# Layer 1's products are no longer added in pairs, and the expert work, the scatter's side work and the first steps change their order

## The reference

```python
xn = layernorm(x)
# layer 0: 32 chunks of 16 tokens, one after the other, for 8 x 16 heads
k_h = softmax(k_t @ W_in) * lr ; q_h = softmax(q_t @ W_in)
o_t = q_h @ W_out + (q_h @ k_h.T * mask) @ v_t
W_out, W_in = W_out + k_h.T @ v_t + ..., W_in + ...       # two updates by attention
s = (layernorm(o) * (xn @ Wg)) @ Wo
x = x + s * silu(moe0(xn))                                # top 2 of 8, gated experts
xn = layernorm(x)
# layer 1: state space scan, 256 channels x 16 states n, 8 batch rows of 512 tokens
h = silu(conv4(xn @ W_in)) ; res = silu(xn @ W_res)
dlt, Bm, Cm = split(h @ W_x) ; delta = softplus(dlt @ W_dt + b)
state[n] = exp(delta * A[n]) * state[n] + delta * h * Bm[n]    # along the tokens
y = sum over n of state[n] * Cm[n] + h * D
s = (y * res) @ W_out
x = x + s * silu(moe1(xn))                                # top 2 of 8, relu, capacity 640
```

## Time and profile before

| | |
|---|---|
| median of three runs | 1483.17 us (1479.82 to 1483.81) |
| profiled execution: its time | 1483.56 us |
| its span, first to last instruction | 1481.8 us |
| instructions | 15782 |
| layer 0, attention steps | from 169.60 us to about 800 us |
| layer 1, row 0 to row 7 | from about 879 us to 1451.83 us |

### The profile page before, as it was taken

How to read it: one execution, slowest core, us unless ns; L and a number is a source line. 1 busy time by engine, 2 the same in 40 slices (tenths; PEclk the granted TensorE clock), 3 DMA queues, 4 the chain that set the end, 5 groups by cost and what they waited for, 6 DMA issues and landing times. The chain is left out here.

```text
span 1481.8 us, 15782 instructions
## 1 busy us (share of the span) xinstructions
PE 982.6 (66%) x3548; PEld 573.3 (39%) x3549; DVE 1267.5 (86%) x2435; ACT 706.7 (48%) x1337; POOL 692.2 (47%) x630
## 2 busy tenths in 40 slices
PE   3670125877878787777534675379888898987531
PEld 1140123555555555555324521134434444443200
DVE  5768986999999999999998888399989898899944
ACT  2542212555555455555322263068678576784305
POOL 5003772222222222222110037639888898888770
PEclk9875556889898889988757588579999999999955
DMA  9993111000000000000522133145454453544741
GB/s 369 220 185 54 36 47 25 21 20 21 21 21 18 20 20 20 19 18 11 144 85 57 29 121 124 57 144 163 155 185 167 153 188 125 187 139 151 162 51 57
DMA packets 94436, 141.23 MB, mean 95 GB/s; under 512 B 22068, under 2 KB 66881, under 8 KB 89905
## 3 DMA queue, kind: packets, MB, share of 16 engines
q1 hardware_dynamic: 83696, 118.01, 26.8%
q0 software_dynamic: 10688, 22.67, 5.7%
HBM read 108.02 MB, written 34.74 MB: 96 GB/s over the span
## 5 line engine op out<-in xcount | busy, mean ns | idle before, releaser
L1919 DVE TENSOR_TENSOR ps<-ps,cv 128x512 f32<-128x512 f32 x256 | 162.9, 682 | 27.3 <-ACT ps L1451 27.3
L1034 PE MATMUL ps<-Q,ident 128*128 128x512 f32 x256 | 143.7, 654 | 49.4 <-issue 24.8
L757 POOL TENSOR_TENSOR Q<-LR,xn 128x512 f32<-128x512 f32 x96 | 122.1, 1272 | 57.5 <-DVE LR L1928 42.2
L723 POOL DMA_INDIRECT y_tok<-xnT,meta x72 | 75.5, 1049 | 151.4 <-ACT xnT L1204 143.4
L700 POOL DMA_INDIRECT slots_x<-xn,sl_put x64 | 74.6, 1165 | 130.2 <-DVE sl_put L1575 111.1
L873 PE MATMUL ps<-wd_a,xn 128*128 x576 | 99.5, 325 | 36.7 <-ACT xn L1198 36.7
L497 POOL TENSOR_TENSOR x<-x 128x512 f32<-128x512 f32 x28 | 32.9, 1175 | 188.1 <-DVE x L1721 188.1
L738 POOL DMA_INDIRECT slots_x<-xn,sl_put x64 | 65.0, 1015 | 103.4 <-DVE sl_put L1588 84.2
L883 PE MATMUL ps<-x,ident 128*128 128x64 f32 x512 | 72.3, 293 | 58.7 <-issue 46.4
L856 PE MATMUL ps<-wg_a,xnT 128*128 x144 | 97.2, 763 | 11.3 <-issue 10.0
L873 PEld LDWEIGHTS ps<-wd_a,xn 128*128 128x128 f32 x576 | 83.8, 224 | 50.5 <-issue 49.0
(11 more groups left out here) (337 smaller groups left out, 2813.2 us busy)
## 6 DMA issues: line engine op xcount, KB each, us to landing
cv<-bc_scr SPq DMA_DIRECT2D x64, 512.0 KB
xn<-bc_scr SPq DMA_DIRECT2D x28, 1024.0 KB
qkv_scr<-cv SPq DMA_DIRECT2D x24, 256.0 KB, 6.0
slots_x<-O POOLq DMA_DIRECT2D x18, 260.0 KB, 8.8
xnT<-slots_x SPq DMA_DIRECT2D x72, 64.0 KB, 1.8
x<-in_x SPq DMA_DIRECT2D x8, 512.0 KB, 6.0
O<-bc_scr SPq DMA_DIRECT2D x4, 1024.0 KB
wu_a<-in_w_e SPq DMA_DIRECT2D x12, 256.0 KB, 4.0
```

The lines of the kernel that those rows point to most:

```text
L723: pool.indirect_dma_start(out=y_tok, out_offset=bass.IndirectOffsetOnAxis(ap=meta_bits[:, n, 0:1], axis=0), in_=yg[:, k, :], in_offset=Non ...
L757: pool.tensor_tensor(yc_g0[:, n % 4, :], st_g0[:, n % 2, :], cn, ALU.mult).then_inc(yc_ready, 1)
L1034: pe.matmul(ps[:, 4, :], ident[:], yc_g0[:, n % 4, :], start=(n == 0), stop=(n == NS - 1)).then_inc(y0_used, 1)
L1919: tt(dBu(g), ps[:, 2 + g, :], b_rows[:, n % 4, :], ALU.mult).then_inc((inject0, b_used)[g], 1)
```

## The change

Seven edits, all of order and buffers, save that 42 additions of GpSimd are gone and 42 matmuls are new.

1. `FIRST` is 4: the routed steps begin one step later, one more step is alone, and there is one unrouted step fewer behind them.
2. On TensorE step 31 and `o_mean(1, 0)` stand ahead of `attention_out(0..5)`. On VectorE the products with the gates follow step 31.
3. Row 1 takes Cm from the buffer `c_first`, and s1 of row 0 goes into `wproj`, so `c_load(1, ·)` needs no wait on the scatter. The loads of the first two experts stand in SP's row 1 at n = 4. Pieces begin in row 1 at n = 6: 10 in row 1, 21 in rows 2 and 3, 20 in rows 4 to 6 (before: 19 in rows 1 to 4, 18 in rows 5 and 6).
4. GpSimd does delta_sum and delta_h of row 1 after 48 of the 64 scatters, and then the other 16.
5. Rows 1 to 6 have no additions of pairs, `sum_g1` takes 16 terms in every row, and the g = 1 products have four buffers (also in rows 0 and 7).
6. The stores and the further loads of the experts are issued by ScalarE, behind its own last piece of an expert: 8 stores and 18 loads.
7. ScalarE's dh_copy stands ahead of `taps1` and the piece at n = 15, and VectorE's `finish(c - 1)` stands at n = 2.

```diff
-FIRST = 3
+FIRST = 4
...
-        ye_g1 = r.take(L)
...
+        yo_g1 = yo_g1[:, 0, :], yo_g1[:, 1, :], flat(seg[:])[:, 0:L], nrm[:, 0, :]
...
-            return c_later if c else c_first
+            return c_later if c > 1 else c_first
...
-        s1 = O[:].rearrange("p e t -> p (e t)")
+        s1_later = O[:].rearrange("p e t -> p (e t)")
+        def s1_of(c):
+            return s1_later[:, c * L:(c + 1) * L] if c else wproj[:]
...
+        ROW1_START = 6
...
-        UNITS = NS // 2 + 1
-        def units(c):
-            return NS if own(c) else UNITS
-        def units_before(c):
-            return NS + (c - 1) * UNITS if c else 0
-        def unit_ready(c, u):
-            if own(c):
-                return product(c, 1, u)
-            if u < UNITS - 2:
-                return y_paired, (c - 1) * (UNITS - 2) + u + 1
-            return product(c, 1, u + NS - UNITS)
         def piece_units(c, n):
             if own(c):
                 return ()
-            twice = (2, 11, 13) if c <= 4 else (11, 13)
-            q = (c - 1) * 19 - max(c - 5, 0) + n + sum(m < n for m in twice)
+            if c == 1:
+                return (n - ROW1_START,) if n >= ROW1_START else ()
+            twice = (2, 6, 9, 10, 11) if c <= 3 else (2, 6, 9, 11)
+            q = NS - ROW1_START + (c - 2) * 20 + min(c - 2, 2) + n + sum(m < n for m in twice)
             return (q, q + 1) if n in twice else (q,)
+        def expert_parts(e):
+            k = e % 2
+            return ((w_e1[k], d["w_e1"][e * P:(e + 1) * P, :]), (flat(w_e2[k]), d["w_e2"][:, e * FC * D:(e + 1) * FC * D]),
...
-            def expert_loads(e, k):
-                sp.dma_start(w_e1[k], d["w_e1"][bass.ds(e * P, P), :]).then_inc(e1_loaded[k], 16)
-                sp.dma_start(flat(w_e2[k]), d["w_e2"][:, bass.ds(e * FC * D, FC * D)]).then_inc(e1_loaded[k], 16)
-                sp.dma_start(xg1[k], slots_x1[bass.ds(e * CAP, CAP), :].rearrange("(i p) c -> p i c", p=P)).then_inc(e1_loaded[k], 16)
-            def expert_store(e):
-                sp.wait_ge(moe_out, e * PIECES + PIECES)
-                sp.dma_start(slots_y1[bass.ds(e * CAP, CAP), :].rearrange("(i p) c -> p i c", p=P), yg1).then_inc(y1_stored, 16)
+            def first_experts():
+                sp.wait_ge(scattered1, 16 * 2 * NT)
+                for e in range(2):
+                    for dst, src in expert_parts(e):
+                        sp.dma_start(dst, src).then_inc(e1_loaded[e], 16)
...
+                        first_experts()
                     if n == 7 and c < LAST:
                         bc_store(c + 1)
                     if n == 9:
...
-                            sp.wait_ge(scattered1, 16 * 2 * NT)
-                            for k in range(2):
-                                expert_loads(k, k)
                         c_load(c + 1, 0)
                     if n == 14 and c < LAST:
                         b_load(c + 1, 0)
-                    for q in (piece_units(c, n - 1) if n else piece_units(c - 1, NS - 1) if c else ()):
-                        e, p = divmod(q, PIECES)
-                        if p == PIECES - 1:
-                            expert_store(e)
-                            if e + 2 < E:
-                                expert_loads(e + 2, e % 2)
             bc_store(0)
...
             pool.wait_ge(slots_ready, 2)
             pool.wait_ge(xn_ready, 2 * NT)
             for i in range(NT):
+                if i == 3 * NT // 4:
+                    for g in range(GD):
+                        delta_sum(1, 1, g)
+                    for g in range(GD):
+                        delta_h(1, 1, g)
                 for j in range(2):
                     pool.indirect_dma_start(out=slots_x1, out_offset=bass.IndirectOffsetOnAxis(ap=sl_put[:, j, i:i + 1], axis=0),
                                             in_=xn[:, i, :], in_offset=None, bounds_check=E * CAP - 1,
...
-                    u = n // 2 if n < NS - 2 else n - NS + UNITS
-                    whole = n % 2 or n >= NS - 2
-                    y = yo_g1[(units_before(c) + u) % 3] if whole else ye_g1
                     pool.wait_ge(scanned, c * (GD * NS) + (GD * n + 2))
-                    if whole:
-                        pool.wait_ge(y1_used, units_before(c) + u - 2)
-                    else:
-                        since(pool, y_paired, (c - 1) * (UNITS - 2) + u)
-                    pool.tensor_tensor(y, st_g1[:, n % 2, :], cn, ALU.mult).then_inc(yc_g1_ready, 1)
-                    if n % 2 and n < NS - 2:
-                        pool.wait_ge(*product(c, 1, n))
...
                 step(c, False)
+            step(NCH - 1, False)
+            o_mean(1, 0)
             for g in range(6):
                 attention_out(g)
-            step(NCH - 1, False)
-            o_mean(1, 0)
             o_variance(1, 7)
...
-                pe.wait_ge(*unit_ready(c, u))
-                pe.matmul(ps[:, 5, :], ident[:], yo_g1[(units_before(c) + u) % 3], start=(u == 0), stop=(u == units(c) - 1)).then_inc(y1_used, 1)
+                pe.wait_ge(*product(c, 1, u))
...
-                if own(c):
-                    sum_g1(c, NS - 2 + n)
-                else:
-                    for u in ((UNITS - 3, UNITS - 2), (UNITS - 1,))[n]:
-                        sum_g1(c, u)
...
-                pairs = {n: (n // 2 - 2,) for n in range(4, NS, 2)}
...
-                    for u in (each if own(c) else pairs).get(n, ()):
+                    for u in each.get(n, ()):
...
             step(AFTER + 1, False, early=first_deviation)
             step(AFTER + 2, False, early=decay_rates, late=lambda: oT_scale(range(6)))
-            step(AFTER + 3, False)
...
+                if p == PIECES - 1:
+                    act.wait_ge(moe_out, q + 1)
+                    act.dma_start(slots_y1[e * CAP:(e + 1) * CAP, :].rearrange("(i p) c -> p i c", p=P), yg1).then_inc(y1_stored, 16)
+                    if e + 2 < E:
+                        for dst, src in expert_parts(e + 2):
+                            act.dma_start(dst, src).then_inc(e1_loaded[e % 2], 16)
...
+                    if c < LAST and n == NS - 1:
+                        for g in range(GD):
+                            dh_copy(r, t, g)
...
                         piece(q)
-                if c < LAST:
-                    for g in range(GD):
-                        dh_copy(r, t, g)
             def dh_copy(r, s, g):
...
             step(AFTER + 2, False)
-            step(AFTER + 3, False, late=lambda: gates(range(6)))
             step(NCH - 1, False, last=True)
+            gates(range(6))
             o.wait()
...
-                dve.wait_ge(y1_used, units_before(c) + units(c))
...
-                    tt(yo_g1[(units_before(c) + n) % 3], st(n, 1), cn, ALU.mult).then_inc(own_g1, 1)
+                    since(dve, y1_used, c * NS + n - 3)
+                    tt(yo_g1[(c * NS + n) % 4], st(n, 1), cn, ALU.mult).then_inc(own_g1, 1)
...
                     scan(n, 1)
-                    if n == 1 and c:
+                    if n == 2 and c:
                         finish(c - 1, t)
```

## The result

The changed kernel takes 1488.79 us (median of 19 runs, 1478.18 to 1494.67) where the kernel before took 1479.82 in as many beside it: a ratio of 1.0052, 95% interval 1.0036 to 1.0067. It is slower by half a per cent. The forecast was 1468, faster, with a range up to 1487.

What follows compares the result with a forecast made beforehand. VectorE was taken to set most of the span, with TensorE and GpSimd within 7% in rows 2 to 6. 1481.8 - 16.2 - 0.5 - 19 + 23 - 2.5 = 1466.6 of span, plus 1.8: 1468 us, range 1441 to 1487.

Steps and rivals of the forecast that it cites:

- Edits 1, 2, 3 and 4: First steps -16.2 us, order at the attention's end -0.5, row 0 -19 (with the fourth buffer), VectorE's stalls there 13.8, not 32.8.
- Rival C: Row 0: stopping the scatters does not free TensorE; gain 2.6 us, not 19; 1484.8, no change; chance 0.16.
- Edit 5: Rows 2 to 6: TensorE becomes the bound; 30.1 us for sums, 6.2 for pieces, less waits: +23, 66 us per row.
- theory P: Experiments' expectation: TensorE's 42 more sums are the loss, 0.86 us each; without them 30 us come back in rows 2 to 6.
- Rival B: TensorE's waits in rows 2 to 6 shrink to 5 us a row instead of 10: 25 less, 1443; chance 0.24.
- Edit 6: ScalarE's 26 issues between pieces, partly in its idle time: 1.0 us a row, 5 in all, within the +23.
- rival S: ScalarE's issues cost 1.6 us each, 41.6 instead of 5: 1505, slower from 0.93 each; chance 0.12 including growing TensorE waits.
- Edit 7: Moving dh_copy ahead saves nothing where TensorE is the bound; finish at n = 2 costs 0, in row 7 too.
- Tail: Row 7's four stalls with the gather, 22.5 us: the fourth buffer gives -2.5, bounds -6 and 0.

Runs made afterwards that it cites:

- first_three: Changed kernel with FIRST set back to 3, the step left over standing unrouted before step 31; 1.0144 of the kernel before, in B.
- B: Kind of place for runs, known only by its time: the kernel before takes about 1441 us there; the changed kernel, unchanged, took 1442.19 us, 1.0022.
- gather_pause_again: Changed kernel with GpSimd's 64 gathers of row 7 stopped halfway until VectorE's g = 0 product of state 10; 0.9890 of the kernel before, in A.
- A: Kind of place for runs, known only by its time: the kernel before takes about 1480 to 1485 us there; the changed kernel's ratio is 1.0052.
- finish_at_one: Changed kernel with VectorE's finish at n = 1 again, all else kept; 1471.75 us, 0.9928 of the kernel before, in A.
- pairs_spread_7: Changed kernel with pair additions back, ScalarE's loads spread over pieces 1, 3 and 5, and edit 7 undone; 1444.54 us, 0.9741 of the kernel before, in A.
- pairs_spread: Changed kernel with pair additions back and ScalarE's loads spread over pieces 1, 3 and 5; 0.9747 of the kernel before, in A.
- delta_after: Changed kernel with delta_sum and delta_h of row 1 back behind all 64 scatters; 1.0042 of the kernel before, in B.
- the six profiles: Profiles of the changed kernel (A and B), first_three, delta_after and the paused gathers (both places), alike in rows 2 to 6: 338.6 to 342.5 us.

## Why the prediction was wrong

**Edits 1, 2, 3 and 4: right.** -19.2 for -16.7 before row 0, of which edit 1 is 15.1 by first_three (16.2 forecast), so that 4.1 are left for edit 2 and chance (0.5 forecast; in B the stretch gains 16.7); -20.4 for -19 in row 0, with the release some 5 us after the 48th scatter, the delta operations done at 931 (954 was forecast on the clock of before, from which 21.6 us of earlier start are to be taken) and 16 scatters without a stall. The stalls left, 4.10, 2.24, 3.45 and 2.43 for decays, are 12.2 in sum where 13.8 was written. What I hadn't seen is that SP's wait was worth as much as the delta operations: in B, up to 9.1 and 5.5 us. Rival C is refuted twice, by row 0 and by gather_pause_again. I had put a rule of the Trainium skill beside it ("SBUF — State Buffer", section "Who interferes with whom"), that DMA never contends with a compute engine. It speaks of the ports of SBUF; that the stops freed VectorE in A does not refute it, since in B the same transfers bring no late waits. Taking from it that a stop would free nothing was too much. Whether contention or the delivery of signals makes the waits of A, no run shows.

**Edit 5: right.** TensorE becomes the bound, a row has 68.5 us (64 to 68 was written), and pairs back give the time back. The sum had 30.1 us more work for the 35 sums and 13 less of waits, 17 together; measured are 28.2 to 30.9 of work, 8.7 to 12.9 less of waits, 15.7 to 19.5 together. It was my expectations (theory P), not the forecast, that took the 30.1 in full. Rival B, waits of half that size, did not come: with nothing else undone rows 2 to 6 were 40 longer. The parts as measured one by one, 18.5 for the sums, 10.4 for the issues, 5.9 to 9.8 for finish, -5.9 for dh_copy and the forecast's 6.2 for the pieces, make 35 to 39 of the 40.1; that they add like this across A and B is argued, not shown, and each has the spread of single profiles.

**Edit 6: 5 us taken, 10 to 11 measured.** The place was right and the size half. An issue costs 0.49 in a group of four, not 1.6: rival S had the mechanism and needed 0.93. By the Trainium skill ("DMA: Bandwidth & Descriptors", section "Issuing engines are not separate DMA queues") the time to issue is usually small relative to the transfer. The trace agrees, 0.5 us beside a median of 4.0 from issue to landing for the loads; but that it would then cost about 0 does not follow: 12.9 us of ScalarE's queue in groups cost nearly their sum, and nothing when spread out.

**Edit 7: the step that failed.** It read: "`finish` at n = 2 moves yt_ready by 3.4 us later, while out_proj stands at n = 3 of a TensorE that trails; 0, and in row 7 too." The runs showed 5.9 to 9.8 us in rows 2 to 6 and 13.0 in row 7, some 18 in the kernel's time. TensorE trails at that place in rows 2, 3, 4 and 6, but not in rows 1, 5 and 7: there its work ahead of out_proj is done and out_proj is next, and it waits for finish, 9.46, 2.02 and 10.31 us. What makes finish later then makes out_proj, s1's copy and all later sums later, and the idle time costs clock besides (3.41 instead of 1.95 us for row 5's out_proj). With that one line back the kernel took 1471.75 us where 1468 was forecast, faster (0.9928) and not slower. Since other terms also missed, in both directions (the issues by +5, dh_copy the other way), coming so near 1468 is partly luck. The same part took dh_copy's move as 0; by one profile it is a gain of 10.3, since VectorE still waits for ScalarE's dh_copy at the row's start (36.7 us without the move, 17.8 with it), TensorE-bound or not.

**Tail: -2.5 taken, +9.3 measured.** In A row 7 was 109.5 to 111.6 in the four kernels with finish at n = 2 and all gathers in one piece, and 98.6 to 104.2 in the three with it at n = 1 (before, finish_at_one, pairs_spread_7). The fourth buffer has no part in it; its -2.5 did not come. In B both are 78. So finish's place is shown to make the difference, by 6.6 (pairs_spread to pairs_spread_7, with dh_copy moved too) to 13.0; how a later out_proj makes the stalls with the gathers begin earlier (VectorE's first of over 4 us at 1399.2, 54 us into row 7; before at 1415.6, 66 us in) is open, and so is what differs between A and B.

**Best versions.** Pairs back and issues spread, 0.9741 in A; pairs back, SP issuing and edit 7 undone, 0.9778 in B. Pairs back with finish at n = 1, dh_copy ahead and the gathers paused was not run.

## What to carry to other kernels

When work moves to an engine that then becomes the bound, every other edit must be priced again for that engine: a step that is free while it waits anyway (finish one state later, four issues in a row on the engine that feeds it) is paid nearly in full, and an idle stretch can be paid again in clock. Before costing a move at nothing "because that engine trails", read what stands last and next on it at that very place, and in every row: it trailed in four rows and stood waiting in three. And test each small edit of a bundle by itself: here one line turned a gain of 0.7% into a loss of 0.5%.

## What was unexpected of the hardware

- The same kernel took 1433 or 1482 us of span by place; of the 49 us of difference 24 lie in row 7 (78.8 against 102.3) and 15 in row 0 (93.6 against 108.9), where GpSimd issues 64 indirect transfers beside TensorE's sums. In A VectorE's waits for those sums end late, mostly 5 to 11 us apart (10.5 to 11.2 in row 0 of the kernel before), and the last ends 3 to 7 us after the transfers stop.
- The clock behind a wait differs between executions of the same instructions: the four 512-column sums behind s1's copy took 3.60 us after a wait of 3.15 (row 4, the changed kernel), 1.98 after one of 3.18 (row 4, gather_pause_again) and 3.56 after one of 2.94 (row 2, delta_after). The length of the wait alone does not decide it; what does, no run shows. The 4 us by which the six profiles of rows 2 to 6 differ go with it: 338.6 to 338.8 with no such place in rows 2 and 4, 340.0 and 340.5 with one, 342.5 with two.
- A transfer issued on ScalarE took 0.49 us on average in groups of four and 0.37 alone.
